# A decoder block of 32 sequences: new order of all engines, down product in two halves, set-up by TensorE and ScalarE

## The reference, cut to what matters

```
x = x + attn(layernorm(x))       # RWKV-like: 32 heads of 16, decay per head
x = x + xattn(layernorm(x), ctx) # softmax attention over 128 context rows, 32 query heads on 8 key heads
x = x + ffn(layernorm(x))        # 512 -> 2048 -> 512, both products on quantised operands

# attn: four mixes of x with the token before it, then r, k, v, g = mix @ W.T + b
#   y = ((r @ k) * Wm) @ v ;  Wm[s,t] = w**(t-s-1) below the diagonal, the head's bonus on it
#   y = groupnorm per head(y) * silu(g) ;  out = y @ Wo.T + bo
# ffn: mx_quant on blocks of 32 along the contraction:
#   scale = 2**(floor(log2(max|block|)) - 6) ; q = clip(round(x / scale), -128, 127) * scale
#   h = bf16(quant(ln(x)) @ quant(W1).T + b1) ; h = gelu(h) ; h = bf16(quant(h) @ quant(W2).T + b2)
```

## Time and profile before

| | us |
|---|---|
| median of 3 runs (1512.36 to 1515.04) | 1513.65 |
| the profiled execution | 1511.13 |
| its span, first to last instruction | 1509.3 |

### The profile page before, as it was taken

The page is one execution under the profiler, slowest core; times in us unless marked ns, Lnnn a source line. Parts: engine busy times, 40 slices in busy tenths (PEclk is TensorE's granted clock), DMA queues, the critical chain, the costliest instruction groups (busy, mean ns, idle before and its releaser), DMA issues.

```text
span 1509.3 us, 30585 instructions
## 1 busy us (share of the span) xinstructions
PE 1307.9 (87%) x11491; PEld 838.6 (56%) x11552; DVE 1252.4 (83%) x2060; ACT 812.0 (54%) x1735; POOL 553.0 (37%) x606
## 2 busy tenths in 40 slices
PE   2658799999999999999999999999989999999753
PEld 2535566655556666555556666555556665556421
DVE  5868788888889888888889888888888888887775
ACT  3323455655655655556655655556655555565441
POOL 3424333333334433433334433433334434233221
PEclk9879899999999999999999999999999999999977
DMA  8333211111111011111110011111120111111112
GB/s 271 85 86 80 59 21 28 35 35 35 35 28 25 19 35 35 35 35 35 31 31 21 23 35 35 35 35 35 28 35 9 34 35 33 35 36 28 19 33 45
DMA packets 150833, 62.78 MB, mean 42 GB/s; under 512 B 137632, under 2 KB 139040, under 8 KB 149920
## 3 DMA queue, kind: packets, MB, share of 16 engines
q1 hardware_dynamic: 150688, 60.83, 17.7%
HBM read 26.73 MB, written 8.39 MB: 23 GB/s over the span
## 4 chain that ended last, share of the span: by engine, by line
PE 40%; issue 25%; DVE 17%; DMA 7%; POOL 5%; ACT 3%; SPq 2%; POOLq 0%; DVEq 0%; ACTq 0%
PE bank_b L396 14%; PE bank_a L396 7%; PE rt L454 4%; DMA out<-x 3%; POOL gmem L2875 3%; PE bank_y L419 3%; DMA gmem<-w 2%; PE rt L406 2%; DVE gmem L1458 2%; POOL x L2880 2%; DVE mix_v L1304 2%; PE bank_y L433 2%; PE bank_y L500 1%; DVE amax_g L1400 1%; PE bank_o L480 1%
## 5 line engine op out<-in xcount | busy, mean ns | idle before, releaser
L2880 POOL TENSOR_TENSOR x<-x,o_bf 128x512 f32<-128x512 f32 x32 | 37.0, 1157 | 455.7 <-DVE o_bf L1472 455.7
L1327 DVE TENSOR_TENSOR att<-rt,wm 128x2048 f32<-128x2048 f32 x64 | 146.5, 2290 | 23.2 <-PE rt L406 21.4
L1356 DVE TENSOR_REDUCE negm<-rt 128x16 f32<-128x2048 f32 x64 | 146.2, 2285 | 6.2 <-PE rt L454 6.1
L500 PE MATMUL bank_y<-w2q,gmem 128*128 128x512 bf16 x509 | 118.7, 388 | 37.1 <-DMA gmem<-gmem 36.5
L433 PE MATMUL bank_y<-w_Wo,yT 128*128 128x512 f32 x256 | 120.0, 613 | 29.8 <-DVE yT L1343 29.8
L396 PE MATMUL bank_b<-mix_k,w_Wk 128*128 128x128 f32 x1024 | 125.6, 283 | 18.1 <-DVE mix_k L1304 18.1
L2875 POOL TENSOR_TENSOR gmem<-gmem,unit_g 128x1024 bf16<-128x1024 bf16 x64 | 122.5, 1915 | 48.0 <-DVE unit_g L1406 47.8
L396 PEld LDWEIGHTS bank_b<-mix_k,w_Wk 128*128 128x128 f32 x1024 | 123.9, 201 | 21.3 <-DVE mix_k L1304 10.7
L2332 ACT ACTIVATE pT<-rt 128x2048 f32<-128x2048 f32 x64 | 119.6, 1868 | 17.2 <-PE rt L467 11.7
L396 PE MATMUL bank_a<-mix_r,w_Wr 128*128 128x128 f32 x1024 | 124.7, 281 | 0.0
L396 PEld LDWEIGHTS bank_a<-mix_r,w_Wr 128*128 128x128 f32 x1024 | 119.7, 196 | 5.2 <-issue 2.2
(11 more groups left out here) (167 smaller groups left out, 2814.0 us busy)
## 6 DMA issues: line engine op xcount, KB each, us to landing
...
```

The source lines that it names most:

```text
L500: done = e.matmul(bank_y[:, :], gqT[:, t, :], w2q[:, t, :], start=(t == 0), stop=(t == FT - 1))
L1327: e.tensor_tensor(att[:, :, :, :, :].rearrange("p g m a t -> p (g m a t)"), rt[:, :], wm[:, i, :, :, :, :].rearrange("p g m a t -> p (g m ...
L1356: e.tensor_reduce(negm[:, 0:H].rearrange("p (g i j) -> p g i j", g=4, i=2)[:, :, i, :], rt[:, :].rearrange("p (g j s) -> p g j s", g=4, j= ...
```

## The change

**Down in two tasks.** `down(n)` becomes `down(n, 0)` and `down(n, 1)`, each of 8 matmuls into the same accumulation, each waiting for its own half. `gelu_turned(n, i)` waits for `pe_down{i}`, and `second_out` for `pe_down1` and, new, for `pool_y`.

**Scale bits.** `block_floor` and `block_pow2` work on the upper 16 bits of each 32-bit maximum (stride two), and write `unit` and `pow2` as bf16.

**Set-up.** PE centres Wv and its bias by 20 matmuls with a centring matrix, ACT copies the result to `wt["Wv"]` and `bv_row`; ACT writes the bonuses as scaled diagonals into `rt` (32 instructions), and DVE adds them to `wm` in two. Identity, head means, centring matrix, distances and parity come in one load, decays and bonuses in one.

**w1q.** It is laid out as [P, 16, 4, 128], so that a piece of W1 is turned by one DMA rather than two; a matmul of `up` reads 4 runs of 128 columns rather than 512 adjacent ones.

**Orders.** All five lists are new. The loop is `range(10, 29)`, and a turn of it begins behind `down`. ACT's turn now has gelu in two places and four table loads instead of two.

```diff
             def gelu_turned(n, i):
                 e.wait_ge(sem(f"dve_gq{i}"), n + 1)
                 if n:
-                    e.wait_ge(sem("pe_down"), n)
+                    e.wait_ge(sem(f"pe_down{i}"), n)
...
-                    done = e.matmul(bank[:, :], hqT[:, c, :], w1q[:, c, j * C:(j + 1) * C],
+                    done = e.matmul(bank[:, :], hqT[:, c, :], w1q[:, 4 * j:4 * j + 4, c, :],
                                     start=(c == 0), stop=(c == KT - 1))
...
-            def down(n):
-                e.wait_ge(sem("sp_gqT0"), 16 * (n + 1))
-                e.wait_ge(sem("sp_gqT1"), 16 * (n + 1))
+            def down(n, i):
+                e.wait_ge(sem(f"sp_gqT{i}"), 16 * (n + 1))
...
-                for t in range(FT):
+                for t in range(8 * i, 8 * i + 8):
                     done = e.matmul(bank_y[:, :], gqT[:, t, :], w2q[:, t, :], start=(t == 0), stop=(t == FT - 1))
-                done.then_inc(sem("pe_down"), 1)
+                done.then_inc(sem(f"pe_down{i}"), 1)
...
+            def centre_values():
+
+                e.wait_ge(sem("sp_Wv"), 16)
...
+                for f in range(KT):
+                    for c in range(KT):
+                        at = f * C + c * P
+                        e.matmul(rtb(c)[:, f * P:(f + 1) * P], wv_rows[:, at:at + P], centre[:, :], start=True, stop=True)
...
             def block_pow2(key, name, n):
                 e.wait_ge(sem(name), n)
-                bits = amax[key][:, :].bitcast(I32)
-                e.tensor_scalar(pow2[key][:, :].bitcast(I32), bits, EXP_BITS, None, ALU.bitwise_and)
-                return e.tensor_scalar(unit[key][:, :].bitcast(I32), bits, EXP_BITS, EXP_BITS,
+                bits = upper(amax[key][:, :])
+                e.tensor_scalar(pow2[key][:, :].bitcast(U16), bits, EXP_BITS, None, ALU.bitwise_and)
+                return e.tensor_scalar(unit[key][:, :].bitcast(U16), bits, EXP_BITS, EXP_BITS,
                                        ALU.bitwise_and, ALU.bitwise_xor)
...
+            def bonus_added(i):
+                e.wait_ge(sem("act_wm"), i + 1)
+                e.wait_ge(sem("act_diag"), i + 1)
+                half = wm[:, i, :, :, :, :].rearrange("p g m a t -> p (g m a t)")
+                e.tensor_tensor(half, half, rt[:, :], ALU.add).then_inc(sem("dve_wm"), 1)
```

ACT's turn, one of those written out behind the loop (gelu 0 and 1 stood behind the queries' norm before, and now stand ahead of the cross attention's norm):

```diff
             weights_x(26, 1)
+            keys_r(28)
+            e.preload_act_table_set(TABLE_GELU)
+            gelu(25, 0)
+            gelu(25, 1)
+            e.preload_act_table_set(TABLE_EXP)
             rstd_log("x", 27)
             rstd_exp("x", 27)
             normalise_x(27)
             out_x(26, 1)
             rstd_log("q", 29)
             rstd_exp("q", 29)
+            keys_x(27)
             normalise_q(29)
-            e.preload_act_table_set(TABLE_GELU)
-            gelu(25, 1)
-            x_turned(29)
-            gelu(25, 0)
```

1878 lines of the change are left out of this document (955 added, 923 removed).

## The result

| | before | after |
|---|---|---|
| median of 4 runs, us | 1514.35 | 1416.73 |
| lowest and highest | 1512.36, 1515.32 | 1413.17, 1419.89 |
| profiled execution, its span | 1511.13, 1509.3 | 1419.46, 1417.7 |
| after / before (95% interval) | | 0.9356 (0.9326 to 0.9387) |

The account below looks back on a forecast made before the run. PE was taken to bound the loop, with 2.71 us of waits in a turn of 42.50. From 1511.1, -36 (19 loop turns), -7 (written-out turns), -0 (ramp) and -3 (tail) gave 1465; median 1467.5, range 1446 to 1500.

Parts of the forecast that it names:

- 1.14 + 1.05 - 0.3: Loop: the two waits of PE go, less 0.3 us of new costs; a turn gains 1.9 us and takes 40.6.
- PE's two waits: Loop: project_out waits for gated_y, 1.14 us a turn, and down for the DMA transposes, 1.05; both were to go.
- The four tight places: Loop: four places where new waits could form, together taken as 0.3 us a turn, bounds 0 and 1.2.
- (a): Loop, first quarter of up behind project_out: it needs the hidden values, there at 3.3 to 3.7 us; cost 0 to 0.5.
- (b): Loop, turn_keys_queries: waits for xq behind ACT's two gelus and two table loads, but PE covers it; cost 0.
- (c): Loop, values_r behind down: needs second_out over, which stands behind decayed on DVE; cost 0 to 0.3 us.
- one wait stays: Rival, loop: one of the two waits stays or a new one replaces it; a turn gains 0.9, 1490 us; chance 0.20.
- forecast 0, bounds -9 and +13: Ramp: the end of W1's last piece, on which the first gelu waits, moves between 9 us sooner and 13 later; 0 taken.
- One transpose instead of two for a piece of W1 is hidden in SP's queue: Ramp, SP: turning each piece of W1 by one transpose rather than two was given no gain.
- the 10.3 us of DVE work: Ramp, DVE: loses means_removed (6.4 us) and bonuses (8.48), gets two adds (4.6); 10.3 us less.
- forecast -3: Tail, last down: its first half runs before the second half's transposes land; 3 us gained, bounds 0 and 6.
- layout on PE: Rival, up: reading four strided runs costs PE up to 1.03 us more a quarter, 1568 us; chance 0.05.

Follow-up runs that it names:

- a_back: The changed kernel with gelu_quantised of the first half and gelu_max of the second put back on DVE where the kernel before had them: 1431.6 us.
- b_layout: The kernel before with only w1q in the new layout, one transpose for a piece of W1 rather than two: 1506.2 us, ratio 0.9958.
- a_dve_setup: The changed kernel with the set-up by DVE again (head means out of Wv, bonuses in 32 instructions), none of it on PE and ACT: 1415.3 us.

## Why the prediction was wrong in its size

**Loop (forecast 1.9 us a turn, 43 us in 26 turns; measured 3.1 in most turns, 72 us from tile 3 to 28).** The step that failed is the sum "1.14 + 1.05 - 0.3": it took PE's two waits as causes, each with a price. Made alone, their edits gave nothing (1518.5, 1509.8 and 1516.1 us for 1510.8). What the runs show in its place is two closed chains, both through what DVE owes between `decayed(., 1)` and `gated_y`: 13.39 us before, 11.09 after (796.87 to 807.96). The section on the change shows `gelu_quantised` moved behind `gated_y`, but the prediction gave that no price, since in a view of waits it has none; alone it was worth some 27 us. With the split and the move of `stats_q` the chains account for 42.4 to 40.5; the last 1.1 us stay open. That the sum had the right sign and 1.9 of the 3.1 us is luck: the change opened the chains for other reasons, so the two waits did go, and with them all that the sum had kept.

- It kept 39.79 us as PE's work; this was 39.35 in the changed kernel. Part of it was the waits themselves: `a_back`, with PE's order of the changed kernel and 0.8 us of gaps, shows 39.73 busy, since the modelled end of a matmul is later where a wait follows.
- It kept about 0.5 us of short waits; the transposes of x and `up` hardly wait any more.
- It added 0.3 for new waits; there are none in most turns.

0.44 + 0.5 + 0.3 and the 1.9 are the 3.1. The four tight places were seen rightly: `mix_v` is held (560 ns instead of 346, 600 were expected), at (a) PE passes the hidden values without a wait, and neither (b) nor (c) shows. The rival "one wait stays" (0.20) did not come, and no rival of the prediction was faster than the forecast. That was the gap in it: its upper bound of 2.4 us a turn lies below the 2.71 that the earlier trace rows give as PE's idle time, although its words have the short waits gone as well. Where PE has waits everywhere in a turn, its bare work is a bound that the change may reach, 42.5 - 39.4 = 3.1 us a turn as it turned out, and it belonged into the range.

**Ramp (forecast 0, bounds -9 and +13, measured -15 at `first_sum(3)`).** `stats_q` of tile 0 starts at 42.41 (14.25 in the earlier trace rows), as foreseen (42), and tile 0 is 9.6 us late. Two steps failed. One dismissed a term: "One transpose instead of two for a piece of W1 is hidden in SP's queue" (`b_layout`, in the kernel before: 9 us by `first_sum(3)`, of which 5 last to the end). The other counted one that isn't there: the 10.3 us of DVE work (`a_dve_setup`: 0 in the changed order). PE's busy time in the first 200 us, 127 before, was the right thing to watch: it is 137, at a granted clock of 0.88 instead of 0.86. The 6 us of the ramp that `b_layout` doesn't explain I leave to the order of tasks; no run isolates them.

**Tail (forecast -3, measured -4 from `first_sum(28)` on).** The size is right by luck, the mechanism only half: 5.3 of it come in the turns from 28 to 31, and behind the last `first_sum`, where the forecast looked for its 3 us, the change loses 1.4. SP and PE at the last `down`, which answers the earlier trace rows:

```profile
1403.76 1.23 SPq L217 DMA_TRANSPOSE gmem<-gmem  x1
...
1405.71 1.29 SPq L217 DMA_TRANSPOSE gmem<-gmem  x1
...
1406.94 5.79 PE L511 MATMUL bank_y<-w2q,gmem 128*128 128x512 bf16 x16 [11.62 <-DMA gmem<-gmem]
```

The first half starts 3.2 us behind the issue of its own transpose; the second has landed when it is due. The granted clock is 0.62 in these 5.79 us (0.64 in the 5.57 of before). From the end of the last quantising (1405.33) to the end of the span it is 12.4 us, 13.7 before: 1.3 of the 2.8 us that the split was to give.

**16-bit halves, layout on PE:** nothing, as forecast.
